# Splitting the two indirect sends of a routed tile on GpSimd: one behind k's spreading, one at the end of the step

## The chip, the cores and the metric

The kernel runs on one core of a Trainium2 chip, in a single launch. The metric is the device time in microseconds; the median of three timed runs of the kernel before is 567.29 us (566.72 to 568.52).

The engines are named as in the profile: PE is TensorE (PEld is its weight load), DVE is VectorE, ACT is ScalarE, POOL is GpSimd and SP is SyncE. Each runs its own list of instructions in order, and they meet at semaphores.

## The reference, cut to what matters

A decoder layer over x of 32 sequences, each of 128 tokens with 128 features:

```
x = x + self_attention(layernorm(x))            # 16 heads of 8, window 32, rotary
x = x + cross_attention(layernorm(x), ctx)      # 16 heads of 8, window 16, biases
xn = layernorm(x)
probs = softmax(xn @ gate_w)                    # 8 experts
topw, topi = top_k(probs, 2); topw /= topw.sum()
x = x + sum over the 2 chosen experts of topw * (gelu(xn @ w1[e]) @ w2[e])
```

Both attentions are causal. The kernel computes an expert only for the tokens that chose it, so each token's normalised row is written twice to a buffer in HBM, once for each of its two experts, at a place that is known only at run time.

## The kernel before, in words

One sequence is one tile of 128 tokens on the 128 partitions. Three stages follow each other: self-attention over 32 tiles, cross-attention over 32 tiles (with routing of the finished tiles beside it), and the experts, over 71 blocks of 128 routed rows.

Both attentions are software pipelines. In step c an engine works on several tiles at once: PE makes the scores of tile c+1, turns the probabilities of tile c, projects tile c-1 and makes q and k of tile c+2; DVE normalises tile c+4. In cross-attention the routing trails behind: the third layernorm of tile c-2, the gate's logits of tile c-3, the choice of the top two of a pair of tiles in even steps ("choosing", c-4) and the places of their rows in odd steps ("placing", c-5). Steps that are in the middle of the stage stand in a hardware loop of four steps each (`Fori`); the first and last are written out. An engine's order of work is exactly the order in which its step function is written.

POOL's step (`pool_step`, L642) in cross-attention holds, in this order:

- L662, `k_heads`: k of tile c+2 spread over the four heads of a group (each with zeros at the others). It waits for ACT's q and k (L579, L580) and for the scores that read the previous `k_heads`. PE's next scores (masks at L409, then L416) wait for it through `s_spread`.
- `route_pool` (L868): the two indirect sends of tile c-6, L878, one for each rank k of `TOPK = 2`. Each takes 128 rows of 132 floats from `row[:, t, k, :]` to the slots in `slot_u[:, t, k]`. They wait for `s_slot` (the placing, DVE L950) and `s_rows` (the copy of the rows, ACT L857), and both add to the semaphore `s_sent[t]`.
- L669: the output bias is added to x of tile c+4.
- L680 and L683: the inverse deviation `rstd` for the layernorms, from `mean_var` (DVE L770 and L774). DVE's L707 (`xn`) and L711 (`xn3`) wait for it.

At the end of the stage `LAST_SENDS` (L265) gives the steps B-1, B, B+1 and B+3 the tiles that are left: 26, 27, then 28 and 29, then 30 and 31, each behind the step's `rstd`.

The row buffers and slots are fourfold (`t = tile % 4`). ACT's L857 and DVE's L938 write a buffer again when `s_sent[t]` says that both sends of four tiles ago have landed. After the attention, ACT waits for all `s_sent` and for the padding rows before it reads the first routed rows (L1056), and PE's experts begin with those.

Of the kernel before, what the change touches and what calls it, by code (L numbers as in the profile page):

```python
# [9 lines left out]
B = 32  # L10
# [16 lines left out]
E, F, TOPK = 8, 512, 2  # L27
# [58 lines left out]
def build(nc, x_in, ctxT_in, consts_in, wself_in, wcross_in, cols_in, rows_in, gate_in, w1_in, w2_in, out):  # L86
# [5 lines left out]
    with ctx:  # L92
# [147 lines left out]
        def cv(at, n):  # L240
            return consts[:, at:at + n]

        def x_of(n):
            return x[:, bass.ts(n, P)]
# [20 lines left out]
        LAST_SENDS = {B - 1: [B - 6], B: [B - 5], B + 1: [B - 4, B - 3], B + 3: [B - 2, B - 1]}  # L265
# [23 lines left out]
        def runs(h, c, lead):  # L289

            return not isinstance(h, int) or 0 <= c + lead < B

        def wait(eng, s, value):

            if not isinstance(value, int) or value > 0:
                eng.wait_ge(s, value)

        def plain(eng):

            eng.sem_inc(s_plain, 1)  # L300
# [66 lines left out]
        def attention(kind):  # L367
            base = B * kind
            own = kind == 0
# [7 lines left out]
            def exists(h, c, lead):  # L377

                return not isinstance(h, int) or 0 <= base + c + lead < 2 * B

            def folds_bias(h, c):

                return not own and isinstance(h, int) and c == FIRST
# [258 lines left out]
            def pool_step(h, c):  # L642
                def count(lead):
                    return TURN * h + (c + lead + base)
                if folds_bias(h, c):
                    nc.gpsimd.wait_ge(s_bvo_sb, 1)
                    nc.gpsimd.tensor_tensor(rows[:, P:2 * P], rows[:, P:2 * P], bv_out[:, :], ALU.add).then_inc(s_bias, 1)
                    nc.gpsimd.wait_ge(s_bias, 1)
                if own and runs(h, c, 2):

                    n = count(2)
                    slot = (c + 2) % 2
                    wait(nc.gpsimd, s_qk, n)
                    nc.gpsimd.wait_ge(s_swap[slot], 16 * TURN * h + 32 * ((c + 2) // 2 + 1))
                    plain(nc.gpsimd)
                    nc.gpsimd.tensor_tensor(turned_sin[:, :, :], swapped[:, slot, :, :], cv(C_SIN, P).unsqueeze(1).to_broadcast([P, 2, P]), ALU.mult).then_inc(s_rot, 1)
                if runs(h, c, 2):

                    n = count(2)
                    nc.gpsimd.wait_ge(s_qk, n + 1)  # L660
                    wait(nc.gpsimd, s_scores, 2 * n)
                    nc.gpsimd.tensor_tensor(k_heads[:, :, BLK:], qk[:, 1:2, :].to_broadcast([P, G, P]),  # L662
                                            cv(C_HEAD, G).unsqueeze(2).to_broadcast([P, G, P]), ALU.mult).then_inc(s_spread, 1)
                if not own and (not isinstance(h, int) or c < B):
                    route_pool(h, c, [c - 6])
                yield
                if not own and runs(h, c, 4):
                    nc.gpsimd.wait_ge(s_xn, count(4) + 1)
                    nc.gpsimd.tensor_tensor(x_of(TURN * h + (c + 4)), x_of(TURN * h + (c + 4)), rows[:, P:2 * P], ALU.add).then_inc(s_bo, 1)  # L669
                yield  # L670
                if runs(h, c, 5 + ahead) or (not own and runs(h, c, -1)):

                    n = count(5 + ahead)
                    both = 1 if own else 2
                    nc.gpsimd.wait_ge(s_mv, n + 1)
                    if exists(h, c, 4 + ahead):
                        wait(nc.gpsimd, s_xn, n)
                    if not own and runs(h, c, -2):
                        nc.gpsimd.wait_ge(s_xn3, TURN * h + (c - 1))
                    nc.gpsimd.tensor_tensor(var_eps[:, 0:both], mean_var[:, 0:both, 1:2].squeeze(2),  # L680
                                            eps[:, 0:1].to_broadcast([P, both]), ALU.add).then_inc(s_ve, 1)
                    nc.gpsimd.wait_ge(s_ve, n + 1)
                    nc.gpsimd.tensor_tensor(rstd[:, 0:both], var_eps[:, 0:both], minus_half[:, 0:1].to_broadcast([P, both]), ALU.pow).then_inc(s_rstd, 1)  # L683
                if not own and isinstance(h, int) and c in LAST_SENDS:

                    route_pool(h, c, LAST_SENDS[c])


            def add_result(h, c):
# [36 lines left out]
            def dve_step(h, c):  # L726
# [50 lines left out]
                if runs(h, c, 0):  # L777
# [6 lines left out]
                    nc.vector.tensor_tensor(att[:, :].rearrange("p (h d) -> p h d", d=HD), heads[:, :, 0:HD],  # L784
                                            inv_sum[:, :, :].to_broadcast([P, HEADS, HD]), ALU.mult).then_inc(s_att, 1)
            return pe_step, act_step, pool_step, dve_step

        def n_is_first(n):
# [76 lines left out]
                    a = nc.scalar.activation(ratio[:, t, :], top[:, t, 0:1], ACT.Exp, bias=top[:, t, 1:2], scale=-1.0)  # L865
                a.then_inc(s_ratio, 1)

        def route_pool(h, c, tiles):  # L868

            for tile in tiles:  # L870
                if isinstance(h, int) and not 0 <= tile < B:
                    continue
                t = tile % 4
                nc.gpsimd.wait_ge(s_slot, TURN // 2 * h + tile // 2 + 1)
                nc.gpsimd.wait_ge(s_rows, TURN * h + tile + 1)
                plain(nc.gpsimd)
                for k in range(TOPK):
                    nc.gpsimd.indirect_dma_start(out=sent, out_offset=bass.IndirectOffsetOnAxis(ap=slot_u[:, t, k:k + 1], axis=0),  # L878
                                                 in_=row[:, t, k, :], in_offset=None).then_inc(s_sent[t], 16)

# [352 lines left out]
```

## Time and profile before

| | |
|---|---|
| timed runs, median (range) | 567.29 us (566.72 to 568.52) |
| profiled execution, from its first to its last instruction (its span) | 562.7 us |
| timed median less the span: what lies around it | 4.6 us |
| PE busy | 485.7 us, 86% |
| DVE busy | 372.7 us, 66% |
| ACT busy | 332.5 us, 59% |
| POOL busy | 308.3 us, 55% |
| first and last indirect send of routed rows start at | 232.4 us and 393.6 us |

The page gives the profiled execution by its span, and no other time of it. All starts below are microseconds from the first instruction of that span. Busy shares are averages over three stages with different limits, so each stage is read by itself: its chain of waits (which work ended last, step by step) and its timeline (each instruction's start, duration and, in square brackets, how long its engine sat idle before it and what ended that). "issue" in a bracket means that no semaphore event explains the gap.

### The profile page before, as it was taken

Reading aid. Unit: us, or ns where it says so; the run is one execution under the profiler, and the core shown is the slowest. Engines: PE = TensorE matmul, PEld = TensorE weight load, DVE = VectorE, ACT = ScalarE, POOL = GpSimd, SP = SyncE. Lnnn points to the kernel's source line nnn. Section 1 sums busy time; section 2 is a strip of 40 time slices with the busy share of each in tenths; the row PEclk is TensorE's granted clock in tenths of the full one; section 3 lists DMA queues with packets and bytes.
Section 4 is the critical chain, followed back from the end, with each engine's and each line's share of the span. In section 5 each row is a group of like instructions: output and inputs, shape, how many; then the busy total and the mean of one; then the engine's idle time right before and its main releaser. Section 6 shows DMA issues by size and latency. Waiting matters only on the chain.

```text
span 562.7 us, 30637 instructions
## 1 busy us (share of the span) xinstructions
PE 485.7 (86%) x11903; PEld 400.6 (71%) x11903; DVE 372.7 (66%) x1314; ACT 332.5 (59%) x985; POOL 308.3 (55%) x413
## 2 busy tenths in 40 slices
PE   2689999999999798898999999973799999999930
PEld 2367777777776566676777777751599999999920
DVE  5467888888877355677877777665166666666626
ACT  3367778777786576787888887852134343343400
POOL 2444455445536343577778786767055555555624
PEclk9999999999999898999999999985799999999985
DMA  8211111111110000011111111012222222222139
GB/s 234 77 57 50 47 57 56 48 50 51 56 58 23 13 17 13 23 48 31 38 33 38 33 41 37 28 36 85 48 68 72 67 64 71 65 67 72 48 138 322
DMA packets 40801, 34.93 MB, mean 62 GB/s; under 512 B 6413, under 2 KB 37263, under 8 KB 40736
## 3 DMA queue, kind: packets, MB, share of 16 engines
q1 hardware_dynamic: 24752, 19.62, 11.1%
q0 software_dynamic: 4320, 8.53, 4.6%
q10 hardware_dynamic: 11664, 5.88, 4.4%
q8 instruction: 46, 0.75, 0.6%
q14 instruction: 19, 0.16, 0.1%
HBM read 18.58 MB, written 11.68 MB: 54 GB/s over the span
## 4 chain that ended last, share of the span: by engine, by line
PE 79%; issue 6%; DVE 4%; DMA 3%; SPq 2%; POOL 2%; ACT 1%; ACTq 1%; DVEq 0%; POOLq 0%
PE p_scores L1029 11%; PE p_probsT L533 11%; PE p_att_bank L523 8%; PE p_scores L416 8%; PE p_att_bank L1038 6%; PE p_v_bank L1038 5%; PE p_scores L461 4%; PE p_v_bank L486 4%; PE p_scores L409 4%; PE p_att_bank L471 3%; PE p_qk L437 2%; PE p_qk L428 2%; PE p_v_bank L502 2%; PE p_att_bank L820 2%; SPq L330 2%
## 5 line engine op out<-in xcount | busy, mean ns | idle before, releaser
L662 POOL TENSOR_TENSOR k_heads<-qk,consts 128x512 f32<-128x512 f32 x64 | 66.8, 1044 | 99.8 <-DVE qk L724 58.2
L1114 POOL DMA_INDIRECT expert_results<-weighted,result_at x71 | 75.5, 1063 | 71.5 <-DVE weighted L1102 49.1
L737 DVE TENSOR_REDUCE shift<-p_scores 128x8 bf16<-128x512 f32 (+1 forms) x128 | 74.1, 619 | 24.0 <-PE p_scores L416 23.5
L1078 ACT ACTIVATE hidden<-p_scores 128x512 f32<-128x512 f32 x71 | 42.4, 597 | 78.9 <-PE p_scores L1029 58.7
L560 ACT COPY probsT<-p_probsT 128x512 f32<-128x512 f32 x128 | 75.6, 590 | 21.1 <-PE p_probsT L533 21.0
L533 PE MATMUL p_probsT<-consts,probs 128*128 128x128 f32 x512 | 80.0, 280 | 0.4
L566 ACT ACTIVATE probs<-p_scores 128x512 f32<-128x512 f32 x128 | 78.0, 610 | 0.3 <-PE p_scores L461 0.3
L1029 PE MATMUL p_scores<-gotT,w_now 128*128 128x128 f32 x568 | 76.7, 279 | 1.6 <-ACT gotT L1081 1.6
L878 POOL DMA_INDIRECT sent_rows<-row,slot_u x64 | 64.3, 1005 | 15.8 <-issue 15.8
L1029 PEld LDWEIGHTS p_scores<-gotT,w_now 128*128 128x128 f32 x568 | 70.5, 195 | 1.8 <-ACT gotT L1081 1.8
L619 ACT COPY values<-p_v_bank 32x128 f32<-32x128 f32 x256 | 68.4, 267 | 2.2
L533 PEld LDWEIGHTS p_probsT<-consts,probs 128*128 128x128 f32 x512 | 59.0, 143 | 7.7 <-ACT probsT L560 6.4
L416 PE MATMUL p_scores<-k_heads,qk 32*32 32x256 f32 (+1 forms) x2048 | 60.1, 368 | 3.9 <-issue 3.9
L523 PE MATMUL p_att_bank<-values,probsT 128*32 128x36 f32 x4096 | 55.4, 203 | 4.1 <-issue 3.6
L523 PEld LDWEIGHTS p_att_bank<-values,probsT 128*32 128x32 f32 x4096 | 45.5, 111 | 15.6 <-issue 8.3
L1093 DVE COPY w_now<-w 128x512 f32 x71 | 30.4, 428 | 34.6 <-PE p_scores L1029 29.3
L683 POOL TENSOR_TENSOR rstd<-var_eps,minus_half 128x2 f32<-128x2 f32 (+1 forms) x70 | 44.7, 639 | 5.5
L707 DVE TENSOR_SCALAR xn<-x,mean_var,rstd 128x128 f32 (+1 forms) x64 | 42.9, 671 | 3.3 <-POOL rstd L683 2.9
L696 DVE TENSOR_TENSOR x<-x,p_att_bank 128x128 f32 (+1 forms) x64 | 18.4, 287 | 37.5 <-PE p_att_bank L471 37.5
L1038 PE MATMUL p_att_bank<-w_now,hidden 128*128 128x128 f32 x288 | 39.3, 281 | 0.4 <-ACT hidden L1078 0.4
L409 PE MATMUL p_scores<-masks_bf,ident_bf 32*32 32x256 bf16 (+1 forms) x1024 | 25.8, 269 | 14.3 <-issue 7.8
L461 PE MATMUL p_scores<-shift,minus_ident_bf 128*128 128x256 bf16 (+1 forms) x256 | 37.0, 262 | 0.9 <-issue 0.4
(133 smaller groups left out, 951.6 us busy)
## 6 DMA issues: line engine op xcount, KB each, us to landing
got<-sent_rows ACTq DMA_DIRECT2D x71, 66.0 KB, 1.9
swapped<-raw SPq DMA_DIRECT2D x64, 64.0 KB, 1.9
w<-w_in SPq DMA_DIRECT2D x32, 128.0 KB, 2.3
back<-expert_results SPq DMA_DIRECT2D x8, 512.0 KB, 6.6
ctxT<-ctxT_in SPq DMA_DIRECT2D x32, 64.0 KB, 1.9
out<-x SPq DMA_DIRECT2D x8, 256.0 KB, 5.2
x<-x_in SPq DMA_DIRECT2D x4, 448.0 KB, 9.8
expert_results<-weighted,result_at POOLq DMA_INDIRECT x71, 2.4
```

What stands on the lines that cost most here:

```text
L416: mm = nc.tensor.matmul(p_scores[j * BLK:(j + 1) * BLK, r * G:(r + 1) * G, low:WIN], qk[r * BLK:(r + 1) * BLK, 0, j * BLK:(j + 1) * BLK], ...
L523: mm = nc.tensor.matmul(p_att[j * BLK:(j + 1) * BLK, r * VROW:(r + 1) * VROW], probsT[:, 4 * (r // HALF) + 2 * ks + r % HALF, j * BLK:(j + ...
L533: mm = nc.tensor.transpose(p_probsT[:, i * P:(i + 1) * P], probs[:, half, ks, r * G:(r + 1) * G, :].rearrange("p g k -> p (g k)"), ident)
L560: nc.scalar.copy(probsT[:, 4 * half:4 * half + 4, :], p_probsT[:, :].rearrange("p (m q) -> p m q", q=P)).then_inc(s_pT, 1)
L566: nc.scalar.activation(probs[:, half, :, :, :].rearrange("p s h k -> p h s k"), p_scores[:, half * 8:half * 8 + 8, 0:WIN].rearrange("p h ( ...
L619: a = nc.scalar.copy(values[lo:lo + BLK, slot, 1:, :, g, 0:HD], p_v[lo:lo + BLK, :].rearrange("p (b r d) -> p b r d", b=NBLK, d=HD))
L662: nc.gpsimd.tensor_tensor(k_heads[:, :, BLK:], qk[:, 1:2, :].to_broadcast([P, G, P]), cv(C_HEAD, G).unsqueeze(2).to_broadcast([P, G, P]), ...
L737: nc.vector.tensor_reduce(shift[:, half * 8:half * 8 + 8], p_scores[:, half * 8:half * 8 + 8, low:WIN], AX.X, ALU.max).then_inc(s_max, 1)
L878: nc.gpsimd.indirect_dma_start(out=sent, out_offset=bass.IndirectOffsetOnAxis(ap=slot_u[:, t, k:k + 1], axis=0), in_=row[:, t, k, :], in_o ...
L1029: mm = nc.tensor.matmul(p_hidden[half][:, f * P:(f + 1) * P], w1_now[:, half, f * P:(f + 1) * P], gotT[:, half, :], start=True, stop=True)
L1038: mm = nc.tensor.matmul(p_y[half], hidden[:, half, f * P:(f + 1) * P], w2_now[:, half, f * P:(f + 1) * P], start=(f == 0), stop=(f == FC - 1))
L1114: nc.gpsimd.indirect_dma_start(out=results, out_offset=bass.IndirectOffsetOnAxis(ap=result_at[:, slot:slot + 1], axis=0), in_=weighted[:, ...
```

## The change

`route_pool` takes the ranks to send. Of the tile c-6 the first rank (0) stays where both were, behind the spreading of k. The second rank (1) goes to the end of POOL's step, behind the inverse deviation. The last six tiles, which `LAST_SENDS` places, still send both ranks together.

```
                 if not own and (not isinstance(h, int) or c < B):
-                    route_pool(h, c, [c - 6])
+                    route_pool(h, c, [c - 6], [0])
                 yield
...
                     nc.gpsimd.tensor_tensor(rstd[:, 0:both], var_eps[:, 0:both], minus_half[:, 0:1].to_broadcast([P, both]), ALU.pow).then_inc(s_rstd, 1)
+                if not own and (not isinstance(h, int) or c < B):
+                    route_pool(h, c, [c - 6], [1])
                 if not own and isinstance(h, int) and c in LAST_SENDS:
 
-                    route_pool(h, c, LAST_SENDS[c])
+                    route_pool(h, c, LAST_SENDS[c], range(TOPK))
...
-        def route_pool(h, c, tiles):
+        def route_pool(h, c, tiles, ranks):
...
-                for k in range(TOPK):
+                for k in ranks:
```

The first place is on POOL, in the loop of cross-attention: one step before, from the spreading of k (`k_heads`) to the next one (REGISTER_ALU and ISA rows are the sequencer's own).

```order
L662 TENSOR_TENSOR k_heads<-qk,consts 128x4x128 [waits scores_made]
L878 DMA sent_rows<-row,slot_u 38016x132 [waits rows_filled]
L878 DMA sent_rows<-row,slot_u 38016x132
L669 TENSOR_TENSOR x<-x,rows 128x128
L680 TENSOR_TENSOR var_eps<-mean_var,eps 128x2 [waits xn3_made]
L683 TENSOR_TENSOR rstd<-var_eps,minus_half 128x2 [waits var_eps_made]
```

And the same step of the changed kernel, on the same engine.

```order
L662 TENSOR_TENSOR k_heads<-qk,consts 128x4x128 [waits scores_made]
L880 DMA sent_rows<-row,slot_u 38016x132 [waits rows_filled]
L669 TENSOR_TENSOR x<-x,rows 128x128
L680 TENSOR_TENSOR var_eps<-mean_var,eps 128x2 [waits xn3_made]
L683 TENSOR_TENSOR rstd<-var_eps,minus_half 128x2 [waits var_eps_made]
L880 DMA sent_rows<-row,slot_u 38016x132 [waits slots_made,rows_filled]
```

The second send has moved past the bias and both steps of the inverse deviation, and now stands directly ahead of the next spreading.

The second place is on POOL too, at the end of cross-attention (steps 30 to 32): the kernel before, sends of tiles 24, 25, 26 and 27.

```order
L878 DMA sent_rows<-row,slot_u 38016x132 [waits slots_made,rows_filled]
L878 DMA sent_rows<-row,slot_u 38016x132
L680 TENSOR_TENSOR var_eps<-mean_var,eps 128x2 [waits xn3_made,mean_var_made]
L683 TENSOR_TENSOR rstd<-var_eps,minus_half 128x2 [waits var_eps_made]
L878 DMA sent_rows<-row,slot_u 38016x132 [waits slots_made,rows_filled]
L878 DMA sent_rows<-row,slot_u 38016x132
L680 TENSOR_TENSOR var_eps<-mean_var,eps 128x2 [waits xn3_made,mean_var_made]
L683 TENSOR_TENSOR rstd<-var_eps,minus_half 128x2 [waits var_eps_made]
L878 DMA sent_rows<-row,slot_u 38016x132 [waits slots_made,rows_filled]
L878 DMA sent_rows<-row,slot_u 38016x132
L680 TENSOR_TENSOR var_eps<-mean_var,eps 128x2 [waits xn3_made,mean_var_made]
L683 TENSOR_TENSOR rstd<-var_eps,minus_half 128x2 [waits var_eps_made]
```

The changed kernel there ("x2" is two such rows in a row).

```order
L680 TENSOR_TENSOR var_eps<-mean_var,eps 128x2 [waits xn3_made,mean_var_made]
L683 TENSOR_TENSOR rstd<-var_eps,minus_half 128x2 [waits var_eps_made]
L880 DMA sent_rows<-row,slot_u 38016x132 [waits slots_made,rows_filled] x2
L680 TENSOR_TENSOR var_eps<-mean_var,eps 128x2 [waits xn3_made,mean_var_made]
L683 TENSOR_TENSOR rstd<-var_eps,minus_half 128x2 [waits var_eps_made]
L880 DMA sent_rows<-row,slot_u 38016x132 [waits slots_made,rows_filled] x2
L880 DMA sent_rows<-row,slot_u 38016x132
L680 TENSOR_TENSOR var_eps<-mean_var,eps 128x2 [waits xn3_made,mean_var_made]
L683 TENSOR_TENSOR rstd<-var_eps,minus_half 128x2 [waits var_eps_made]
```

Between the deviation of step 31 and that of step 32 three sends now stand where two stood: the second of tile 25 and both of tile 26.

## Rows read from the trace of the kernel before

**Rows 1.** The page: the chain that ended last, by engine.

```profile
PE 79%; issue 6%; DVE 4%; DMA 3%; SPq 2%; POOL 2%; ACT 1%; ACTq 1%; DVEq 0%; POOLq 0%
```

**Rows 2.** PE in one turn of four steps: window, length, busy (instructions), granted clock, DMA.

```profile
289.00:311.50 22.50, 21.83 (x681) 1.00 0.11 36
```

**Rows 3.** Timeline of POOL, one step of the loop: start, duration, instruction.

```profile
300.30 1.04 POOL L662 TENSOR_TENSOR k_heads<-qk,consts 128x512 f32<-128x512 f32 x1 [0.61 <-ACT qk L580]
301.51 1.06 POOL L878 DMA_INDIRECT sent_rows<-row,slot_u  x1 [0.17 <-issue]
302.87 0.95 POOL L878 DMA_INDIRECT sent_rows<-row,slot_u  x1 [0.30 <-issue]
303.84 0.46 POOL L669 TENSOR_TENSOR x<-x,rows 128x128 f32 x1
304.25 0.20 POOL L680 TENSOR_TENSOR var_eps<-mean_var,eps 128x2 f32<-128x2 f32 x1
...
305.73 1.06 POOL L662 TENSOR_TENSOR k_heads<-qk,consts 128x512 f32<-128x512 f32 x1 [0.48 <-ACT qk L580]
306.96 1.06 POOL L878 DMA_INDIRECT sent_rows<-row,slot_u  x1 [0.17 <-issue]
```

**Rows 4.** Timeline of DVE and PE in that step and the next.

```profile
298.14 0.18 DVE L774 BATCH_NORM_AGGREGATE mean_var<-stats 128x2 f32<-128x6 f32 x1
302.92 0.48 PE L409 MATMUL p_scores<-masks_bf,ident_bf 32*32 32x192 bf16 x16
303.63 0.18 DVE L774 BATCH_NORM_AGGREGATE mean_var<-stats 128x2 f32<-128x6 f32 x1
305.29 0.35 DVE L707 TENSOR_SCALAR xn<-x,mean_var,rstd 128x128 f32 x1
307.82 0.19 DVE L943 TENSOR_TENSOR mine<-place,onehot 128x32 f32<-128x32 f32 x1
308.36 0.17 DVE L950 CAST slot_u<-slot_f 128x4 uint32<-128x4 f32 x1
```

**Rows 5.** Waits of DVE from 235 to 370 us: in total, times, the longest.

```profile
DVE x L696 <- PE p_att_bank L471: 23.3, 22, 1.8
```

**Rows 6.** Timeline of the one step in which DVE's routing was stretched.

```profile
262.54 0.95 POOL L878 DMA_INDIRECT sent_rows<-row,slot_u  x1 [0.30 <-issue]
262.91 0.48 DVE L943 TENSOR_TENSOR mine<-place,onehot 128x32 f32<-128x32 f32 x1
263.52 0.47 POOL L669 TENSOR_TENSOR x<-x,rows 128x128 f32 x1
263.53 0.49 DVE L948 TENSOR_SCALAR result_no<-result_no 128x4 f32<-128x4 f32 x1
265.17 0.20 POOL L680 TENSOR_TENSOR var_eps<-mean_var,eps 128x2 f32<-128x2 f32 x1 [1.19 <-DVE mean_var L774]
266.36 0.11 PEld L461 LDWEIGHTS p_scores<-shift,minus_ident_bf 128*128 128x128 bf16 x2 [0.30 <-DVE shift L737]
266.83 0.11 PEld L461 LDWEIGHTS p_scores<-shift,minus_ident_bf 128*128 128x128 bf16 x2 [0.35 <-DVE shift L737]
```

**Rows 7.** Timeline of POOL at the end of cross-attention.

```profile
376.82 0.72 POOL L683 TENSOR_TENSOR rstd<-var_eps,minus_half 128x2 f32<-128x2 f32 x1
377.73 1.10 POOL L878 DMA_INDIRECT sent_rows<-row,slot_u  x1 [0.20 <-issue]
380.96 0.19 POOL L680 TENSOR_TENSOR var_eps<-mean_var,eps 128x2 f32<-128x2 f32 x1 [0.88 <-DVE mean_var L774]
382.14 1.10 POOL L878 DMA_INDIRECT sent_rows<-row,slot_u  x1 [0.20 <-issue]
```

**Rows 8.** The chain of waits there: start, duration, what.

```profile
393.64 2.28 DMA sent_rows<-row,slot_u
```

**Rows 9.** PE's first and a later expert block.

```profile
401.68 2.08 PE L1029 MATMUL p_scores<-gotT,w_now 128*128 128x128 f32 x8 [1.60 <-ACT gotT L1081]
410.59 1.06 PE L1029 MATMUL p_scores<-gotT,w_now 128*128 128x128 f32 x8
```

## The prediction

> **What bounds the kernel now.** I read the chain of waits first. It is 79% PE and 2% POOL [rows 1], so POOL's 55% of busy time can't be traded for time one to one. Then I looked at the stage that the change touches, cross-attention from the first send at 232 us to about 370 us, in stretches of one turn of its loop. In one turn of 22.5 us PE is busy for 21.83 us at full clock [rows 2]; that is 5.6 us for a step, and PE sets them. The timelines of the others tell how far they are from being late. POOL sits idle for 0.48 to 0.61 us in such a step, before it spreads k [rows 3]. DVE waits for PE's projection 22 times, 23.3 us in total, about 1 us in each step [rows 5]. The place where POOL can hold up PE is the spreading of k: it ends at 300.30 + 1.04 = 301.34 us, and the masks that wait for it start at 302.92 us [rows 3, 4]. So 1.58 us are to spare, and this is one of the tightest steps of the 24. At the end of the stage it is otherwise: from 382.14 us on POOL has ten sends in a row, the chain of waits runs along them to the last one, which starts at 393.64 us, and from there through its landing, 2.28 us later, to the experts [rows 7, 8]. There POOL is the bound.
>
> **In the loop.** Nothing is added or removed of the work: 64 sends before, 64 after. Per tile POOL passes once more through the waits for slot and rows, both long met (the slots of the pair in hand were made a step earlier). What changes is the order.
>
> - The bias, L669, follows the first send. It starts at about 301.51 + 1.06 = 302.6 us instead of 303.84 us [rows 3]. What it writes is read a whole step later or more, so this earns nothing.
> - `var_eps` is now ready to start before its input is there. Before, `mean_var` ended at 303.63 + 0.18 = 303.81 us and POOL came to it at 304.25 us, 0.44 us late [rows 3, 4]. Where POOL has waited for it, it starts 0.16 us behind its end (`mean_var` 265.01 us, `var_eps` 265.17 us [rows 6]). So `rstd` comes 0.44 - 0.16 = 0.28 us earlier. I cost this at nothing: `xn` started at 305.29 us, 0.04 us behind `rstd`, but DVE's list has a reduction of the scores right in front of it, and behind it DVE waits for PE for about 1 us [rows 4, 5]. It could be worth at most those 0.28 us in each step.
> - The second send now stands between `rstd` and the next spreading. From `mean_var`: 0.16 of waiting, 0.28 + 0.72 = 1.00 for the deviation (`rstd` takes 0.72 us [rows 7]), 0.20 of gap and 1.06 for a send that follows a tensor operation [rows 3, 7], and a gap ahead of the spreading. This gap isn't in the trace. The gaps beside sends are from 0.02 us (bias behind a send) to 0.30 us (send behind a send); I take 0.10 us. The spreading is then to start at 303.81 + 0.16 + 1.00 + 0.20 + 1.06 + 0.10 = 306.33 us, instead of 305.73 us: 0.60 us later (0.5 to 0.8 by the bounds). One step earlier it is 298.32 + 2.52 = 300.84 us against 300.30 us. Its 1.58 us of room go down to 1.04 us, or 0.8 us at the worst bound. PE doesn't wait, cost 0. If this cover were gone, each further 0.1 us would cost 2.4 us over 24 steps.
> - POOL's whole step is 1.04 + 0.17 + 1.06 + 0.02 + 0.41 + 0.28 + 0.72 + 0.20 + 1.06 + 0.10 = 5.06 us of 5.6 us. It still fits.
>
> The Trainium skill speaks against the new place of the send: by "SBUF — State Buffer", section on two separate sides, a DVE operation in a mode that takes both ports keeps GpSimd from writing descriptors. `xn` and `xn3` come right behind `rstd`, exactly where the second send now stands, and they take 0.35 us each. By that rule the send, and with it the spreading of k, would be up to 0.7 us later again, which leaves 0.3 us of the room: the sum stays as it is, but the rival below gets nearer. The end of the stage already has this pair, a send at 377.73 us beside the `xn3` of that step; it took 1.10 us against 1.06 us [rows 3, 7], so the trace shows 0.04 us of it.
>
> **At the end of the stage.** The sends of tiles 26 to 31 stay where they were, but the second send of tile 25 now stands behind the deviation of step 31, in front of tile 26. Before: `rstd` ends at 377.54 us, two sends to 380.09 us, and POOL sits idle for 0.88 us until `mean_var` lets `var_eps` start at 380.96 us [rows 7]. After: 377.54 + 0.20 + 1.10 + 2 x (0.30 + 0.96) = 381.36 us, and `var_eps` starts at 381.38 us: 0.42 us later. All ten sends behind it, with no idle time between them but the gaps, and so the last landing, move by the same 0.42 us. In the two steps before, one send goes out of and one comes into the space ahead of each `var_eps`, and POOL waits there too in the timeline, so these don't move. The table of blocks, which DVE makes beside them, is ready before the last sends and stays so. Bounds: 0 if the chain to `mean_var` moves too, and 1.26 us, a whole send with its gap, if the idle time had not taken in any of it. I take 0.42 us.
>
> **Sum.** 0 in the loop and +0.42 us at the end. The profiled execution's span of 562.7 us becomes 563.2 us. The timed median lies 4.6 us above the span, for what is around it; with the same 4.6 us it is 567.7 us. Another unknown is PE's clock at the start of the experts: eight matmuls took 2.08 us there at half the clock and 1.06 us later [rows 9]. A start that is moved by 0.4 us can put one block more or less into such a stretch: about 1 us either way. A measurement of this kernel tells 0.3%, 1.7 us, from no change.
>
> **Rivals.**
>
> - *DVE and POOL block each other in the placing steps: slower.* The trace has one step in which it happened. `mine` (L943) took 0.48 us instead of 0.19 us, 0.37 us behind the start of a send, and L948 took 0.49 us, started 0.01 us behind POOL's bias. The scores' maximum was late by those 0.62 us, and PE waited 0.30 + 0.35 us for it [rows 4, 6]. So DVE has next to nothing in hand there, although it idles later in the step. The change moves the first send to 300.84 + 5.49 + 1.21 = 307.54 us in the placing step of [rows 4] (5.49 us is the step, by the two `mean_var`), and `mine` starts at 307.82 us, 0.28 us behind it: near to that case, where before it was 0.86 us behind the send at 306.96 us [rows 3, 4]. The bias comes at 308.62 us, while the cast of the slots ends at 308.53 us: by 0.1 us free. It decides as soon as one of these two operations falls into the other's time in each of the 12 placing steps. One of them costs 0.29 us, less some 0.18 us that the step with both had in hand: 12 x 0.11 = 1.3 us, and 569.0 us; both cost up to 12 x 0.44 = 5.3 us, and 573.0 us. Against it: in the placing step of [rows 4], and in nearly all others, L943 took its 0.19 us. This is the case that the Trainium skill's rule gives ("SBUF — State Buffer", section "Who interferes with whom": a DVE operation with two SBUF inputs blocks against a GpSimd one that reads SBUF, and the later of the two waits for all of the first). The rows agree for the bias and L948, not in full for the sends: most sends ran beside such operations without harm.
> - *The earlier deviation is on a path after all: faster.* In the step of [rows 6] the chain of waits ran through `mean_var`, `rstd` and DVE to PE. If that were so in half of the 24 steps, 12 x 0.28 = 3.4 us go, and with the 0.42 us it is 564.3 us. Against it stands the wait of about 1 us behind `xn` in nearly each step [rows 5].
> - *The send is blocked by both normalisations as in the rule above, and with the gap's worst bound the spreading is late.* 0.24 us of room are left, so this is no change in time, and it is part of the forecast.
>
> **How the numbers follow.** The forecast 70%, its own range 566.0 to 569.0 us (0 to 1.26 us at the end, 1 us of clock, the spread of a median). DVE against POOL 20%, 569.0 to 573.0 us. The earlier deviation 10%, about 564.3 us. The range that leaves out 2 in 10 reaches from the lower part of the third to the near half of the second: 565.6 to 570.3 us. Faster by more than 0.3% means below 565.6 us: the third case and little else, 0.10. Slower means above 569.0 us: the second, 0.20. Within 0.3%: 0.70.
>
> **What would show it.** Right: POOL now waits for `mean_var` before each `var_eps`, by 0.1 to 1 us; the spreading of k starts 0.3 to 0.6 us later against PE's masks, whose distance shrinks to about 1 us and is never used up; a turn of the loop stays at 22.2 to 22.5 us; the last send starts some 0.4 us later against the `mean_var` of step 32. Wrong: PE's masks waiting for `k_heads`; L943, L948 or L950 above 0.25 us in many steps and PE's L461 waiting for the maximum (second case); a turn of the loop shorter by 1 us with less waiting at L696 (third); or an end of the stage that comes earlier than before.

## The result

The changed kernel takes 570.6 us (568.99 to 574.23, 14 runs) where the kernel before takes 567.26 us beside it: a ratio of 1.0062, with a 95% interval of 1.0035 to 1.0088. It is 0.6% slower, about 3.5 us. The forecast was 567.7 us and no change that can be told; the time lies just outside its range of 565.6 to 570.3 us. In a second session the same kernel stood at 1.0154 (1.0095 to 1.0214). The amount itself isn't steady; the experiments show what varies with it. All ratios compare fast runs, those within 1.5% of the fastest of their kernel; two of the six of that second session were slower than that, one of them at 1062.7 us.

The profiled execution of the changed kernel spans 567.1 us, 4.4 us more than before. First its chain of waits by engine, which answers to [rows 1].

```profile
PE 70%; DVE 10%; issue 9%; POOL 3%; DMA 3%; SPq 2%; ACT 1%; DVEq 1%; ACTq 1%; POOLq 0%
```

PE has lost 9 points and DVE has gained 6, POOL only 1. What follows are lines of the table of waits of the changed kernel from 235 to 372 us (in total, times, the longest), which answer to [rows 5].

```profile
POOL var_eps L680 <- DVE mean_var L776: 20.7, 22, 1.6
DVE x L698 <- PE p_att_bank L471: 15.1, 16, 1.8
PEld p_att_bank L445 <- DVE att L786: 4.8, 7, 0.9
PEld p_scores L461 <- DVE shift L739: 3.6, 15, 0.4
PEld p_v_bank L495 <- DVE xn L713: 2.5, 5, 0.6
POOL k_heads L662 <- ACT qk L580: 3.0, 4, 1.0
```

POOL now waits for DVE, as forecast. But DVE no longer waits for PE in every step, and PE waits for three of DVE's results (of `att` 7 times, where the same table of the kernel before has it once, and of `xn`, where it has none): it is DVE that became late. Rows of the timeline of two steps of the changed kernel show with what; they answer to [rows 3] and [rows 4], POOL first.

```profile
301.61 0.72 POOL L683 TENSOR_TENSOR rstd<-var_eps,minus_half 128x2 f32<-128x2 f32 x1
302.52 1.04 POOL L880 DMA_INDIRECT sent_rows<-row,slot_u  x1 [0.19 <-issue]
303.58 1.05 POOL L662 TENSOR_TENSOR k_heads<-qk,consts 128x512 f32<-128x512 f32 x1
304.80 1.01 POOL L880 DMA_INDIRECT sent_rows<-row,slot_u  x1 [0.17 <-issue]
305.84 0.47 POOL L669 TENSOR_TENSOR x<-x,rows 128x128 f32 x1
307.50 0.20 POOL L680 TENSOR_TENSOR var_eps<-mean_var,eps 128x2 f32<-128x2 f32 x1 [1.19 <-DVE mean_var L776]
308.68 1.03 POOL L880 DMA_INDIRECT sent_rows<-row,slot_u  x1 [0.19 <-issue]
```

And DVE and PE in the same two steps.

```profile
302.49 0.34 DVE L709 TENSOR_SCALAR xn<-x,mean_var,rstd 128x128 f32 x1
302.74 1.99 DVE L713 TENSOR_SCALAR xn<-x,mean_var,rstd 128x128 f32 x1
304.79 0.33 PE L495 MATMUL p_v_bank<-consts,xn 128*128 128x128 f32 x1 [0.52 <-DVE xn L713]
305.94 0.31 PE L409 MATMUL p_scores<-masks_bf,ident_bf 32*32 32x192 bf16 x16
307.86 0.33 PE L445 MATMUL p_att_bank<-consts,att 128*128 128x128 f32 x1 [0.38 <-DVE att L786]
308.90 0.34 DVE L713 TENSOR_SCALAR xn<-x,mean_var,rstd 128x128 f32 x1
```

In the first step `xn3` (L713) is issued 0.22 us into the second send and takes 1.99 us instead of 0.34 us. It ends at 304.73 us, 0.10 us behind the spreading of k (303.58 + 1.05 = 304.63 us), which has no gap to the send. PE's transposition L495 waits for it. The next `xn3` is issued 0.22 us into its send as well, and takes 0.34 us. In the timeline from 236 to 372 us I count 7 of the changed kernel's normalisations (xn and xn3) above 1.6 us; before there was none, and two of 0.98 and 1.07 us.

The masks (305.94 us) start 1.31 us behind the end of k's spreading. PE never waits for that.

The last indirect send starts at 398.91 us, 5.27 us later than before, but the span is only 4.4 us longer. The clock that was granted to PE at the start of the experts differs: the eight matmuls that took 2.08 us at a granted clock of 0.50 before [rows 9] take 1.16 us at 1.00 here.

### The profile page after: what moved, and what is told of

It reads as the page before. It is cut to its first block, busy times and chain, and to the rows that moved or that the text cites. A ratio compares the mean times of both kernels' runs of the same rounds, so it can differ in the third digit from the quotient of the medians.

```text
span 567.1 us, 30663 instructions
## 1 busy us (share of the span) xinstructions
PE 481.3 (85%) x11903; PEld 395.3 (70%) x11903; DVE 383.4 (68%) x1314; ACT 334.9 (59%) x985; POOL 310.6 (55%) x413
## 4 chain that ended last, share of the span: by engine, by line
PE 70%; DVE 10%; issue 9%; POOL 3%; DMA 3%; SPq 2%; ACT 1%; DVEq 1%; ACTq 1%; POOLq 0%
PE p_scores L1031 11%; PE p_probsT L533 9%; PE p_att_bank L523 7%; PE p_scores L416 6%; PE p_att_bank L1040 6%; PE p_v_bank L1040 5%; PE p_scores L461 4%; PE p_v_bank L486 3%; PE p_scores L409 3%; PE p_att_bank L471 3%; PE p_qk L428 2%; PE p_v_bank L502 2%; PE p_qk L437 2%; POOL sent_rows L880 2%; DVE x L314 1%
## 5 line engine op out<-in xcount | busy, mean ns | idle before, releaser
L523 PE MATMUL p_att_bank<-values,probsT 128*32 128x36 f32 x4096 | 53.0, 202 | 4.9 <-issue 3.8
L680 POOL TENSOR_TENSOR var_eps<-mean_var,eps 128x2 f32<-128x2 f32 (+1 forms) x70 | 13.7, 195 | 57.0 <-DVE mean_var L776 29.0
L461 PE MATMUL p_scores<-shift,minus_ident_bf 128*128 128x256 bf16 (+1 forms) x256 | 39.1, 263 | 1.0 <-issue 0.4
```

What stands on the lines that cost most here:

```text
L523: mm = nc.tensor.matmul(p_att[j * BLK:(j + 1) * BLK, r * VROW:(r + 1) * VROW], probsT[:, 4 * (r // HALF) + 2 * ks + r % HALF, j * BLK:(j + ...
```

## The experiments

All of them only reorder, or add a wait; nothing is left out in any. Each ratio is against the kernel before in the same session. "Stage" is the time from the first to the last start of 24 spreadings of k, from the one directly ahead of the first send on, in the one profile of each run; before it is 132.3 us, in the changed kernel 136.9 us. The kernel before has a profile in the first session only. By the two later edits that keep its order of deviation and second send, its stage may be up to 2 us longer in another session (134.4 and 133.6 us). The expectations call the first theory A: DVE's xn3 is held back by the second send and the spreading behind it.

**The changed kernel, the second send behind xn3.** Theory A was first tried by keeping the send away from the normalisations.

```
                 if not own and (not isinstance(h, int) or c < B):
+                    if not isinstance(h, int) or 6 <= c < B - 2:
+                        nc.gpsimd.wait_ge(s_xn3, TURN * h + c)
                     route_pool(h, c, [c - 6], [1])
```

> The changed kernel, and in steps 6 to 29 POOL's second send also waits until DVE has made xn3 of the next step (L713 of the changed kernel). Nothing is left out. Theory A (DVE's xn3, issued while the second send runs, waits for it and for the spreading of k right behind it): no xn3 above 0.4 us (7 of 23 took 1.66 to 1.99 us in the changed kernel, 9.2 us of excess), PE no longer waits for xn3 at L495 (2.5 us before), and the time falls by 1 to 3 us, to 568 to 569.5 us. It can't fall all the way, since the spreading and the first send come some 0.5 us later still and may stretch L934 and L950 more. Theory B (the second send makes the spreading of k too late for PE): the send is later by 0.5 us in each step, so PE's masks wait for k, up to 12 us more: over 575 us. Theory C (the bias and the first send, which moved against DVE's routing, are the cost): xn3 is clean, and the time stays at 570 to 572 us.

Measured: 1.0294 (1.0253 to 1.0334), 581.5 us. The normalisations are clean, but the time is that of theory B (over 575 us): I had priced the later spreading at 0.5 us. (The text counts seven stretched xn3; six are xn3 and one is xn.) Its waits from 235 to 364 us:

```profile
POOL sent_rows L882 <- DVE xn L715: 34.7, 20, 3.6
PE p_scores L409 <- POOL k_heads L662: 12.1, 15, 1.0
```

POOL waits for xn3 in 20 steps, 1.7 us each on average, and the send and the spreading come behind it. PE's masks wait for k in 15 steps. The room between the spreading and the masks was 1.56 us at its smallest in the kernel before; here it is gone, and this is the price of the cover that the prediction had named. It isn't the whole of the loss, though: DVE's L944 (0.16 us alone) is now issued 0.33 to 0.49 us into the second send in eight steps, and takes 1.66 to 1.81 us there, up to 0.02 to 0.04 us behind the end of the spreading. The edit took xn3 out of that place and put another operation into it. The run says nothing against theory A, and theory B fails in the next one.

**The changed kernel, k's spreading behind xn3.** The send stays directly behind the deviation.

```
                     wait(nc.gpsimd, s_scores, 2 * n)
+                    if not own and (not isinstance(h, int) or 7 <= c):
+                        nc.gpsimd.wait_ge(s_xn3, TURN * h + (c - 1))
                     nc.gpsimd.tensor_tensor(k_heads[...
```

> The changed kernel, and the spreading of k (L662) also waits until DVE has made xn3 of the step. The second send stays right behind the inverse deviation. Nothing is left out. Theory A: xn3 still has to wait for the send where it is issued into it, but not for the spreading as well: at most some 1.1 us each instead of 1.99 us, and the time is 568.5 to 570 us. Theory B (the spreading late for PE): slower than the changed kernel, since it is later in the steps in which xn3 is stretched. Theory C (bias and first send): as the changed kernel, 570 to 571 us.

Measured: 1.0016 (0.9977 to 1.0055), and the stage takes 129.7 us. This wait gives back the whole loss, more than expected, where theory B had expected a slower kernel. Rows of the timeline of POOL, then of DVE, show that it moves next to nothing:

```profile
298.98 1.03 POOL L882 DMA_INDIRECT sent_rows<-row,slot_u  x1 [0.19 <-ACT qk L580]
300.05 1.05 POOL L664 TENSOR_TENSOR k_heads<-qk,consts 128x512 f32<-128x512 f32 x1
304.11 1.03 POOL L882 DMA_INDIRECT sent_rows<-row,slot_u  x1 [0.19 <-issue]
305.18 1.05 POOL L664 TENSOR_TENSOR k_heads<-qk,consts 128x512 f32<-128x512 f32 x1
```

```profile
299.03 0.34 DVE L711 TENSOR_SCALAR xn<-x,mean_var,rstd 128x128 f32 x1
299.28 0.34 DVE L715 TENSOR_SCALAR xn<-x,mean_var,rstd 128x128 f32 x1
```

The spreading starts 1.07 us behind the start of the send, as in the changed kernel (302.52 to 303.58 us there). The send has the same length, and xn3 is issued into it at 0.30 us. One thing differs here: the spreading can't be taken up before xn3 is done. With that, xn3 takes 0.34 us beside the running send; in four steps, in which xn3 was issued at 0.63 to 0.67 us, the spreading follows the send by 0.12 to 0.13 us instead of some 0.03 us. So it isn't the send alone that holds DVE back for 1.6 us, and not the length of POOL's work; it is a tensor operation that stands ready behind the send. The changed kernel's own profile shows the same within one send.

```profile
314.26 0.36 ACT L580 ACTIVATE qk<-p_qk,cols 128x128 f32<-128x128 f32 x1
314.29 1.03 POOL L880 DMA_INDIRECT sent_rows<-row,slot_u  x1 [0.19 <-issue]
314.57 0.34 DVE L709 TENSOR_SCALAR xn<-x,mean_var,rstd 128x128 f32 x1
314.82 1.67 DVE L713 TENSOR_SCALAR xn<-x,mean_var,rstd 128x128 f32 x1
315.35 1.05 POOL L662 TENSOR_TENSOR k_heads<-qk,consts 128x512 f32<-128x512 f32 x1
```

The spreading waits for ACT's L580, which ends at 314.62 us. xn is issued 0.05 us before that and is free; xn3 is issued 0.20 us behind it and is stretched. So it is in the three profiles that have this order (the changed kernel's two and that of the edit with both sends together from step 29 on). Of the normalisations issued 0.25 us or more into a send with the spreading as its next, 19 took 1.65 us or more, and for each of them L580 had ended 0.19 to 0.68 us before; 16 took at most 0.60 us, and for those L580 ended 0.10 us before at the earliest, mostly later. The rows of L715 over the stage (count: smallest, median, largest in ns) say of all steps that xn3 isn't stretched with the wait, first for this run, then for L713 of the changed kernel.

```profile
L715 DVE TENSOR_SCALAR xn<-x,mean_var,rstd x25: 335/341/437, 237.4 to 370.6; 128x128 f32 x16, 128x128 f32<-128x128 f32 x9
```

```profile
L713 DVE TENSOR_SCALAR xn<-x,mean_var,rstd x23: 334/341/1990, 237.3 to 367.3; 128x128 f32 x16, 128x128 f32<-128x128 f32 x7
```

**The kernel before, with the bias between the two sends.** This moves the first send's neighbour, and the second send stays ahead of the deviation. The cut shows it as an edit of the changed kernel.

```
                     nc.gpsimd.tensor_tensor(x_of(...), ..., rows[:, P:2 * P], ALU.add).then_inc(s_bo, 1)
+                if not own and (not isinstance(h, int) or c < B):
+                    route_pool(h, c, [c - 6], [1])
...
-                if not own and (not isinstance(h, int) or c < B):
-                    route_pool(h, c, [c - 6], [1])
```

> The kernel before with one change: POOL's order is spreading of k, first send, bias, second send, deviation. So the bias (and what it may collide with in DVE's routing) moves as in the changed kernel, by about 1.2 us, and the second send stays ahead of the deviation. Nothing is left out. Theory A (second send beside xn3, then the spreading): xn3 clean, time as before, 567 to 568 us. Theory C (the bias moved onto DVE's routing): L948 and L950 of the kernel before stretched to 0.3 to 0.5 us in the placing steps, 569 to 571 us.

Measured: 1.0013 (0.9979 to 1.0048). The time is as theory A said. xn wasn't clean, though: 9 of the normalisations, issued 0.01 to 0.25 us into the spreading of k itself, took 0.86 to 1.12 us, and eight of DVE's L934 0.45 to 0.62 us, 11.8 us of excess in all by my sum over the timeline. None of it can be told in the time, of which the interval leaves open 2.7 us. The expected stretching of L948 was seen twice only.

**The changed kernel, both sends together from step 29 on.**

```
-                    route_pool(h, c, [c - 6], [0])
+                    route_pool(h, c, [c - 6], [0] if not isinstance(h, int) or c < B - 3 else range(TOPK))
...
-                if not own and (not isinstance(h, int) or c < B):
+                if not own and (not isinstance(h, int) or c < B - 3):
                     route_pool(h, c, [c - 6], [1])
```

> The changed kernel, but from step 29 on both ranks are sent together behind the spreading of k, as in the kernel before; the loop is as in the changed kernel. Nothing is left out. If the end of the stage costs its 0.42 us as forecast, this is 0.4 us faster than the changed kernel, 570.2 us, and 2.9 us slower than before: the loop holds the cost. If the end held most of the cost, it would be within 1 us of the kernel before.

Measured: 1.0179 (1.0132 to 1.0226), slower than the changed kernel's first result, which neither case had foreseen. Its stage takes 143.7 us, and 13 normalisations are above 1.6 us. Here is its xn3 over the stage.

```profile
L713 DVE TENSOR_SCALAR xn<-x,mean_var,rstd x22: 334/1068/1994, 237.9 to 368.1; 128x128 f32 x16, 128x128 f32<-128x128 f32 x6
```

The loop of this kernel is that of the changed one. So either its end did this, or the number of stretched operations isn't fixed by the order. The next run was to tell. (The recorded texts count a few operations of 0.42 to 0.60 us as well, and so come to 8 and 15 where 7 and 13 are above 1.6 us.)

**The changed kernel again, unedited.**

> The changed kernel once more, unedited, beside the others of this call. Theory A2: a tensor operation that stands right behind a send on POOL holds DVE back while the send still runs, if xn or xn3 is issued at 0.22 to 0.56 us into the send; at 0.22 us it goes either way. Then the number of stretched xn and xn3 differs from one execution to the next (8 in the first profile, 15 in the loop of e4_end_together, whose loop is the same), and with it the time: 3 to 10 us above the kernel before. If e4's 1.8% came from its end instead, this kernel is again at 0.6%.

Measured: 1.0154 (1.0095 to 1.0214), 13 normalisations above 1.6 us, stage 140.6 us. The order of the instructions alone doesn't fix the loss.

**The previous edit of k's spreading, again.**

> The same edit as e2_k_after_xn3 (the changed kernel, and the spreading of k also waits for xn3), again, beside the unedited changed kernel. Theory A2: no xn or xn3 above 0.5 us, and as fast as the kernel before within 0.5%; clearly faster than after_again. If e2's result was luck of the run, it is as after_again.

Measured: 0.9978 (0.9945 to 1.0011), none above 0.5 us. In the same session as the run above, one wait is worth 1.8%.

**Only the end changed.** The loop is that of the kernel before, and steps 29 to 31 are split.

```
-                    route_pool(h, c, [c - 6])
+                    route_pool(h, c, [c - 6], [0] if isinstance(h, int) and c >= B - 3 else range(TOPK))
...
+                if not own and isinstance(h, int) and B - 3 <= c < B:
+                    route_pool(h, c, [c - 6], [1])
```

> The kernel before in the loop; only in steps 29, 30 and 31 is the second send behind the deviation. Nothing is left out. The forecast of the end: the last send starts 0.4 us later, 0.4 us slower than before, within what can be measured; the profile is to show three sends between the deviations of steps 31 and 32. If the end holds the cost of the change, 3 us or more slower.

Measured: 0.9989 (0.9953 to 1.0025), no change that can be told. The timeline of POOL at its end, which answers to [rows 7]:

```profile
377.37 0.72 POOL L683 TENSOR_TENSOR rstd<-var_eps,minus_half 128x2 f32<-128x2 f32 x1
378.28 1.09 POOL L880 DMA_INDIRECT sent_rows<-row,slot_u  x1 [0.19 <-issue]
379.68 0.96 POOL L880 DMA_INDIRECT sent_rows<-row,slot_u  x1 [0.30 <-issue]
380.95 0.96 POOL L880 DMA_INDIRECT sent_rows<-row,slot_u  x1 [0.30 <-issue]
382.06 0.19 POOL L680 TENSOR_TENSOR var_eps<-mean_var,eps 128x2 f32<-128x2 f32 x1
...
394.90 0.96 POOL L880 DMA_INDIRECT sent_rows<-row,slot_u  x1 [0.30 <-issue]
```

Three sends stand between the deviations, and `var_eps` follows them by 0.15 us, where it had 0.88 us of idle time before. From the last spreading of k (364.34 us) to the last send it is 30.56 us; before it was 363.54 to 393.64, 30.10 us. The end costs 0.46 us by this measure.

**Both edits together:** k's spreading behind xn3 in the loop, both sends together from step 29 on.

> The edit of e2 in the loop and the edit of e4 at the end (from step 29 on both sends behind the spreading). Nothing is left out. Theory A2: this takes away both of the change's costs; as e2 or 0.4 us faster, and not faster than the kernel before by more than 0.3%, since PE sets the loop's step. If e4's 1.8% came from its end, this is slower than e2_again by several us.

Measured: 0.9976 (0.9934 to 1.0018), stage 130.0 us. It can be told neither from the edit of k's spreading alone (0.9978) nor from the kernel before.

**The changed kernel, with the bias behind the second send.**

```
-                if not own and runs(h, c, 4):
-                    ... (the bias, L669)
...
                     route_pool(h, c, [c - 6], [1])
+                if not own and runs(h, c, 4):
+                    ... (the bias)
```

> The changed kernel with the bias (L669, 0.47 us, its inputs ready long before) moved behind the second send: spreading of k, first send, deviation, second send, bias, spreading of k. Nothing is left out. Theory A2 (the tensor operation right behind a send holds DVE back from about 0.22 us into the send until it is itself done): now the bias does it, not the spreading. So a stretched xn or xn3 ends with the bias: 1.3 to 1.4 us in place of 1.88 to 1.99 us, in the steps where it is issued at 0.22 us or later; 569 to 575 us. Rival A1 (DVE waits for the spreading of k as such, and for whatever is ahead of it): the stretched ones end with the spreading, over 2.3 us. Rival A3 (only the send holds DVE back): at most 1.1 us.

Measured: 1.0043 (1.0001 to 1.0085). The expected 1.3 to 1.4 us was wrong. POOL and DVE in one step:

```profile
288.06 1.03 POOL L880 DMA_INDIRECT sent_rows<-row,slot_u  x1 [0.20 <-issue]
289.12 0.47 POOL L685 TENSOR_TENSOR x<-x,rows 128x128 f32 x1
289.54 1.04 POOL L662 TENSOR_TENSOR k_heads<-qk,consts 128x512 f32<-128x512 f32 x1
```

```profile
288.36 2.30 DVE L709 TENSOR_SCALAR xn<-x,mean_var,rstd 128x128 f32 x1
288.87 1.86 DVE L713 TENSOR_SCALAR xn<-x,mean_var,rstd 128x128 f32 x1
```

xn ends at 290.66 us, 0.08 us behind the spreading of k at 290.58 us, not behind the bias at 289.59 us. DVE waited for the whole train: the rest of the send, the bias and the spreading, which follow each other without a gap. This was the number of the rival that I had called A1, but not for its reason: xn was issued 0.30 us before ACT's L580, which the spreading waits for, had ended (288.66 us), and three more were stretched that were issued 0.23 to 0.40 us before it. Only the bias stood ready then, so the bias began the wait, and the spreading behind it prolonged it. In its timeline eight steps have a normalisation stretched through such a train, about as many as the seven of the changed kernel's first profile, and the two ratios overlap. Its stage is 135.2 us. Three other xn (issued 0.25, 0.38 and 0.55 us into the send) took 0.51 to 0.81 us and ended 0.02 to 0.03 us behind the send, although the bias stood ready behind it; why they got through there isn't known.

**Both sends last.** The first send goes behind the deviation as well.

```
-                if not own and (not isinstance(h, int) or c < B):
-                    route_pool(h, c, [c - 6], [0])
...
-                    route_pool(h, c, [c - 6], [1])
+                    route_pool(h, c, [c - 6], range(TOPK))
```

> The changed kernel with both sends at the end of the step, behind the deviation: spreading of k, bias, deviation, first send, second send. Nothing is left out. xn and xn3 are now issued beside a send behind which another send stands, and the spreading comes 1.26 us later against mean_var. Theory A2: no xn or xn3 above 0.5 us, except where it is issued into the second send; but the spreading is late for PE (the room of 1.1 to 1.6 us is used up), so the time is 4 to 10 us above before for that reason, with PE's masks waiting for k. Rival A3 (a send by itself holds DVE back): xn and xn3 stretched to 0.6 to 1.1 us in most steps.

Measured: 1.0266 (1.0194 to 1.0338), stage 144.9 us. POOL, then DVE and PE; the first rows of each are of one step, the later ones of DVE and PE of the next:

```profile
287.86 1.06 POOL L878 DMA_INDIRECT sent_rows<-row,slot_u  x1 [0.19 <-issue]
289.22 0.96 POOL L878 DMA_INDIRECT sent_rows<-row,slot_u  x1 [0.31 <-issue]
290.21 1.05 POOL L662 TENSOR_TENSOR k_heads<-qk,consts 128x512 f32<-128x512 f32 x1
```

```profile
288.08 0.34 DVE L711 TENSOR_SCALAR xn<-x,mean_var,rstd 128x128 f32 x1
289.64 1.66 DVE L932 TENSOR_SCALAR ratio<-ratio 128x2 f32<-128x2 f32 x1
295.00 0.52 DVE L711 TENSOR_SCALAR xn<-x,mean_var,rstd 128x128 f32 x1
```

```profile
291.40 0.31 PE L409 MATMUL p_scores<-masks_bf,ident_bf 32*32 32x192 bf16 x16 [0.60 <-POOL k_heads L662]
297.94 0.31 PE L409 MATMUL p_scores<-masks_bf,ident_bf 32*32 32x192 bf16 x16 [0.27 <-POOL k_heads L662]
```

With another send behind the send, the normalisations take 0.34 us, at most 0.59 us: four of them, issued 0.49 to 0.59 us into the first send, end 0.02 to 0.03 us behind it. That much is the send's own. The loss is some 15 us, where I had priced it at 4 to 10 us, and k being late is only a part of it: PE's masks waited for k 14 times, 7.1 us in all. The second send now has the spreading behind it, and another operation runs into this place: DVE's L932 (0.16 us alone) took 1.39 to 1.66 us in seven of 11 placing steps, issued 0.41 to 0.69 us into that send, and ended 0.03 to 0.05 us behind the spreading (289.64 + 1.66 = 291.30 us against 291.26 us). It alone is 2% of the chain that ended last. How the 15 us divide between the two isn't shown.

## Why the prediction was wrong, point by point

**The bound.** Right for the kernel before. PE set the loop, but DVE had far less in hand than its 1 us of waiting at L696 suggests: that wait stands behind xn3, and a stretch of 1.6 us uses it up.

**The loop, costed at 0: the deviation, and the second send behind it.** This is the step that failed. I asked only what an earlier `rstd` gains, and whether the send makes the spreading late for PE. I didn't ask what DVE's xn and xn3, which `rstd` releases, now run beside: a send with a ready tensor operation right behind it. Each such meeting stretched a normalisation to 1.65 to 1.99 us. The stage became longer by 4.6 us with 7 of them and by 8.3 us with 13 of them in the two profiles of the changed kernel, some 0.65 us each. Against the edit that has none (129.7 us) it is 7.2 and 10.9 us, 0.8 to 1.0 us each. The second profile's own session has 133.6 us for the loop of the kernel before and 131.3 us for the edit, and against those it is 7.0 and 9.3 us, 0.5 to 0.7 us each. So the price of one is known to 0.5 to 1.0 us only, and in the run with the bias behind the send eight such steps went with a stage just 2.9 us longer than before. That the loss disappears with the stretching, and comes back with the order unedited, is shown by the four runs.

**The pair of the send and the normalisations, 0.04 us.** I weighed the rule of the Trainium skill ("SBUF — State Buffer", section on two separate sides) in one direction only, as a delay of the send, and took its price from the end of the stage. Behind that send another send stood. It was the wrong neighbour: the run with both sends last shows the same pair at 0.34 us, and the loop has the spreading there. The same page says that a GpSimd operation holds the ports for its whole length, and that the other side waits ("Who interferes with whom"). The runs agree on the waiting for the spreading (xn3 ends 0.10 us behind it). In the runs the waiting begins while the send before it is still running (1.99 us), and lasts over two tensor operations in a row (2.30 us).

**Spreading of k later, 0.60 us, not on the path.** Right. The send stands between, the gap ahead of the spreading is 0.02 us (the lower bound, not my 0.10), and the masks come at least 1.07 us behind. The two runs that used up the room lost 2.7 and 2.9%, of which PE's waits for k are a part (7.1 us in 14 steps and 12.1 us in 15).

**The end of the stage, +0.42 us.** About right: 0.46 us from the last spreading on in the run with the end alone, 0.58 us in the changed kernel (368.23 to 398.91 us). It can't be told in the timed runs (0.9989, 0.9953 to 1.0025). **The clock at the experts, 1 us either way.** It went the good way in the profile: the last send is 5.27 us later and the span 4.4 us longer.

**The rival of DVE and POOL.** It named the engines, the sign and, with 1.3 to 5.3 us, the size, but the wrong instructions; that the measured 570.6 us lies in its range is luck. L945 (`mine`, L943 before) was stretched once. L948, which I had put under the rule for two SBUF inputs, has one, so its row doesn't bear that rule out. L934, L942, L950 and others had some 6 us of excess together in the changed kernel; the edit that isn't slower has about 7 us of it, so these stretches cost little or nothing. A rival can be right in time for a reason that isn't there.

**The rival of the earlier deviation.** It may have a gain that the loss hides. With the stretching gone the stage is 2.6 and 1.0 us shorter than before in the two profiles of the first such edit and 2.3 us in that of both edits together. The timed runs can't tell it (1.0016, 0.9978 and 0.9976, all three intervals hold 1).

## What to carry to other kernels

When a step on GpSimd is moved, list for each of its old and new neighbours what VectorE starts there, in both directions: what it does to the send, and what it does to VectorE. A price for such a pair from another place of the trace holds only if the same kind of instruction stands behind it. Where a VectorE operation is released by GpSimd, and GpSimd then goes on with a send and a tensor operation, a wait of the tensor operation for that VectorE operation may be nearly free: here it cost GpSimd 0.1 us in four steps and took back the whole loss. Then look for the VectorE operation that now stands in the place of the one that was moved: in two of the edits another one was stretched there.

## What the runs showed of the hardware

A tensor operation that stood ready directly behind an indirect send on GpSimd held back VectorE's operations while the send was still running: xn and xn3 in the changed kernel, L944 and L932 in two of the edits. A stretched xn or xn3 was issued from 0.22 us after the start of the send on, and ended 0.08 to 0.10 us behind the last of GpSimd's tensor operations without a gap between them (an xn3 behind a stretched xn up to 0.15 us): 1.99 us over the rest of a send and one operation, 2.27 to 2.39 us over the rest of a send and two. Issued at 0.21 us or less it was always free. From 0.25 us on it depended on whether the spreading's last input was there: 19 stretched with it there for 0.19 us or more, 16 not stretched with it there for 0.10 us at most or not yet. At 0.22 and 0.23 us it went either way even with the input there for 0.25 us or more, in the same loop, from turn to turn and from run to run (14 stretched, 8 free in the three profiles). The profile with 7 stretched ones is of the session that measured 1.0062, that with 13 of the session that measured 1.0154. What decides it at 0.22 us is left open, and so is how the waiting tensor operation acts so early: only its effect was measured.
